# The last group of a factorization-machine kernel: rows of the result added into PSUM banks, the last block copied by ScalarE, four stores in place of three

## The chip, the cores and the metric

One Trainium2 chip, one of its cores. The metric is the time of one execution on the device in microseconds (us); lower is better. Before the change the median of 3 runs is 777.99 us (777.85 to 778.26).

## The reference, cut to what matters

```python
B, N, H, L = (2048, 512, 1024, 8)          # x is r_x, (2048, 512), float32
s = jnp.einsum('bn,hln->bhl', x, beta)
ssq = jnp.einsum('bn,hln->bhl', x * x, beta * beta)
fm = 0.5 * jnp.sum(s * s - ssq, axis=-1)
linear_out = x @ W.T + b
return fm + linear_out
```

The output has 2048 rows and 1024 columns, float32.

## The kernel before, in words

The work is ten passes, each a product of x (or x squared) with a matrix of 512 rows and 1024 columns: one pass for W, eight for beta (a chunk of 128 values of h with their eight l each), and a last one, pass 9 (`Q_PASS`), for x squared times the sums of beta squared over l, scaled by -0.5. A pass takes the 2048 rows in eight pairs of 128-row blocks (`PAIRS`). One pair in one pass is a *group* `g`; there are 80 groups, and the last pass holds groups 72 (`FIRST_Q`) to 79 (`GROUPS - 1`).

A group is one multiplication of 2 x 2 blocks by seven block products and not eight. The two row blocks and the two 512-column halves give four result blocks, called 11, 12, 21 and 22 (row block first). Each float32 operand is split into a high and a low part (`t_hi`, `t_lo`, `s_hi`, `s_lo`), and each product is three matmuls of the parts times two halves of the contraction (`KP`), so six matmuls (lines 442, 446 and 448) of 128 x 128 by 512 columns. A group has 42 of them.

The products of a group use four PSUM banks, one set for even and one for odd groups. TensorE makes, in this order, P5 in bank E, P7 in bank D, P1 in bank A, P6 in bank B, and then adds three more onto banks that are kept: P3 onto E, P4 onto D, P2 onto A (`start` is False there, so the matmul accumulates). The helper `whole(g, place, s_op, t_op, start)` issues one product. The waits of TensorE ahead of P3, P4 and P2 say that whoever needed P5, P7 and P1 alone has taken them. The semaphores `p5_made`, `p7_made` and so on tell that a product is finished. With R2 = P1 + P6 (`add_r2`, line 804, from ScalarE's copy `r1` of P1, line 606, and bank B) the blocks are:

- 11 = bank A at its end (P1 + P2)
- 12 = bank E at its end (P5 + P3) + R2
- 21 = bank D at its end (P7 + P4) + R2
- 22 = P5 + P7 + R2

In the last pass the other nine passes' result is already in a buffer `f` in SBUF (`f_at(i)`, i = g - 72; for the last two groups it lies in the tile `cs`), two rows of blocks by 1024 columns, and each group adds its four blocks onto `f` and stores `f` to `out`. For groups 73 to 78 VectorE does, in this order: P5 onto `f` 22 (line 904), P7 onto `f` 22 (line 908), R2 (line 804), block 11 of the group before (`add_o11`, line 838), bank E onto `f` 12 (line 924), bank D onto `f` 21 (line 928). GpSimd, which does not read PSUM, adds R2 onto `f` 12, 21 and 22 (lines 987, 988, 996). The additions of VectorE at 924 and 928 wait for GpSimd's at 987 and 988. In the last group, 79, VectorE does GpSimd's two itself (lines 919 and 920), GpSimd does only 22 (line 996), and block 11 (line 838) comes after everything else.

SyncE issues all transfers. `store_rows(g)` stores block 12 (256 KB, line 347), then the row 21 and 22 in one (512 KB, line 350), then block 11 (256 KB, line 352), each after the semaphore of its sum; at its end SyncE waits until all stores have landed. In the last group SyncE, ScalarE and GpSimd have nothing else to do but what is named here; ScalarE's last instruction is the copy of P1 into `r1`.

The order of work on each engine is written out by hand as the order of the instructions in its block; nothing plans it at run time.

Of the kernel before, what the change touches and what calls it, by code (L numbers as in the profile page):

```python
# [5 lines left out]
P = 128  # L6
B, N, H, L = 2048, 512, 1024, 8
COLS = 512
PAIRS = B // (2 * P)
# [25 lines left out]
GROUPS = PAIRS * (Q_PASS + 1)  # L35
# [24 lines left out]
def pair_of(g):  # L60
    return order_of(g // PAIRS)[g % PAIRS]
# [6 lines left out]
def count(g):  # L68

    return g - DIRECT + 1  # L70
# [45 lines left out]
def fm_layer(nc, x_p, beta_p, w_p, bias, out):  # L116
# [12 lines left out]
    with ExitStack() as ctx:  # L129
# [3 lines left out]
        def sem(name):  # L133
            return ctx.enter_context(nc.semaphore(name))
# [87 lines left out]
        f12_added = sem("f12_added")  # L222
        f21_added = sem("f21_added")
        o22_added = sem("o22_added")

        block = ctx.enter_context(nc.Block())

# [34 lines left out]
        def _(sp):  # L262
# [72 lines left out]
            def load_f(i):  # L335
                last = FIRST_Q - PAIRS + i
                sp.wait_ge(acc_stored[last % 2], 16 * ((last - FIRST_MAIN) // 2 + 1))
                if i >= 6:
                    sp.wait_ge(rows_summed, FIRST_Q - FIRST_MAIN - 1 + i % 2)
                sp.dma_start(f_at(i), acc_kept.rearrange("(t p) h -> p t h", p=P)[:, 2 * i:2 * i + 2, :]  # L340
                             ).then_inc(f_loaded[i], 16)

            def store_rows(g):
                i, rows = g - FIRST_Q, 2 * pair_of(g) * P
                f = f_at(i)
                sp.wait_ge(c12_added, count(g))
                sp.dma_start(out[rows:rows + P, COLS:], f[:, 0, COLS:]).then_inc(stored, 16)
                sp.wait_ge(c21_added, count(g))
                sp.wait_ge(o22_added, i + 1)
                sp.dma_start(out[rows + P:rows + 2 * P, :], f[:, 1, :]).then_inc(stored, 16)  # L350
                sp.wait_ge(o11_added, i + 1)
                sp.dma_start(out[rows:rows + P, 0:COLS], f[:, 0, 0:COLS]).then_inc(stored, 16)
# [60 lines left out]
            for g in range(FIRST_Q, GROUPS):  # L413
# [11 lines left out]
                    load_f(5 + i)  # L425
                if i:
                    store_rows(g - 1)
            store_rows(GROUPS - 1)
            sp.wait_ge(stored, 48 * PAIRS)

        @block.tensor
        def _(pe):
# [18 lines left out]
            def whole(g, place, s_op, t_op, start):  # L451

                n = g // PAIRS
                for k in range(KP):
                    ready = t_split_place(n, t_op, k) if g % PAIRS == 0 or g <= DIRECT else None
                    made = product(bank(g, place), slot_of(g), s_op, t_hi[:, n % 2, t_op, :, :],
                                   t_lo[:, n % 2, t_op, :, :], k, start and k == 0, k == KP - 1, ready)
                return made
# [46 lines left out]
            for g in range(DIRECT, GROUPS):  # L505
                n, i = g // PAIRS, g % PAIRS
                if g in PREPARED:
                    pe.wait_ge(s_lo_ready, s_split_place(g))
                elif i >= HALF:
                    pe.wait_ge(s_loaded[slot_of(g)], 32 * (n if slot_of(g) >= 2 else n - 1))  # L510
                wait_bank(g, BANK_E)
                whole(g, BANK_E, S1, T1, True).then_inc(p5_made, 1)
                wait_bank(g, BANK_D)
                whole(g, BANK_D, S3, T3, True).then_inc(p7_made, 1)
                wait_bank(g, BANK_A)
                whole(g, BANK_A, A11, B11, True).then_inc(p1_made, 1)
                wait_bank(g, BANK_B)
                whole(g, BANK_B, S2, T2, True).then_inc(p6_made, 1)
                if g <= FIRST_Q:
                    pe.wait_ge(r5_copied, count(g))  # L520
                else:
                    pe.wait_ge(p5_taken, g - FIRST_Q)
                whole(g, BANK_E, S4, B22, False).then_inc(p3_made, 1)
                if g <= FIRST_Q:
                    pe.wait_ge(r7_copied, count(g))
                else:
                    pe.wait_ge(p7_taken, g - FIRST_Q)
                whole(g, BANK_D, A22, T4, False).then_inc(p4_made, 1)
                pe.wait_ge(r1_copied, count(g))
                whole(g, BANK_A, A12, B21, False).then_inc(p2_made, 1)  # L530

        @block.scalar
        def _(act):
# [56 lines left out]
            def square_x(g):  # L590
                act.wait_ge(x_loaded[slot_of(g)], x_loads(g))
                nc.scalar.activation(x_at(g)[:, 0:4, :], x_at(g)[:, 0:4, :], ACT.Square).then_inc(x_squared, 1)
# [95 lines left out]
            for g in range(FIRST_Q, GROUPS):  # L688
                for other in groups_for(SUMMED_IN, g):
                    split_s(other)  # L690
                copy_r1(g)
                for other in groups_for(SQUARED_IN, g):
                    square_x(other)

        @block.vector
        def _(dve):
# [196 lines left out]

            for g in range(FIRST_Q, GROUPS):
                i = g - FIRST_Q
                f = f_at(i)
                for other in groups_for(SUMMED_IN, g):
# [14 lines left out]
                add_r2(g)  # L914
                if i:
                    add_o11(g - 1)
                if g == GROUPS - 1:
                    dve.wait_ge(r2_added, count(g))
                    nc.vector.tensor_tensor(f[:, 0, COLS:], f[:, 0, COLS:], r2[:, :], ALU.add).then_inc(f12_added, 1)  # L919
                    nc.vector.tensor_tensor(f[:, 1, 0:COLS], f[:, 1, 0:COLS], r2[:, :], ALU.add  # L920
                                            ).then_inc(f21_added, 1)
                dve.wait_ge(p3_made, count(g))
                dve.wait_ge(f12_added, i + 1)
                nc.vector.tensor_tensor(f[:, 0, COLS:], bank(g, BANK_E), f[:, 0, COLS:], ALU.add
# [2 lines left out]
                dve.wait_ge(f21_added, i + 1)  # L927
                nc.vector.tensor_tensor(f[:, 1, 0:COLS], bank(g, BANK_D), f[:, 1, 0:COLS], ALU.add  # L928
                                        ).then_inc(c21_added, 1)
            add_o11(GROUPS - 1)  # L930

        @block.gpsimd
        def _(pool):
# [90 lines left out]
```

## Time and profile before

| | us |
|---|---|
| median of 3 runs | 777.99 (777.85 to 778.26) |
| the profiled execution | 779.09 |
| its span, first to last instruction | 777.3 |
| TensorE busy | 771.2 (99%) |
| VectorE busy | 572.2 (74%) |
| ScalarE busy | 395.2 (51%) |
| GpSimd busy | 343.3 (44%) |

The profile is of one execution. Its span runs from the first to the last instruction; what the execution takes beyond it, 1.8 us, lies around the instructions. In the rows PE is TensorE's matmul, PEld its loading of weights (beside the matmuls), DVE is VectorE, ACT ScalarE, POOL GpSimd, SPq the queue on which SyncE issues transfers. L904 is line 904. Matmul durations overlap: one starts 0.22 to 0.23 us after the other, and each is shown as 0.39 long. The granted clock of TensorE is full over the whole span.

### The profile page before, as it was taken

The numbers are of one execution on the slowest core, as the hardware profiler recorded it, in microseconds if no ns is written. First come the engines' busy times: TensorE is split into PE (matmuls) and PEld (weight loads), VectorE is DVE, ScalarE is ACT, GpSimd is POOL, SyncE is SP. The second block draws the span as 40 slices with busy tenths as digits, with TensorE's granted clock in tenths as the row PEclk, the third lists the DMA queues.
The fourth block names the chain that finished last, engine by engine and source line by source line (L and its number), as shares of the span: only waits on it lengthen the run. The fifth ranks groups of instructions, "written<-read, shape, count | busy, mean of one in ns | idle before, by whom it ended". The sixth has DMA issues, their size and how long they took to land.

```text
span 777.3 us, 9620 instructions
## 1 busy us (share of the span) xinstructions
PE 771.2 (99%) x3382; PEld 633.5 (82%) x3382; DVE 572.2 (74%) x582; ACT 395.2 (51%) x502; POOL 343.3 (44%) x264
## 2 busy tenths in 40 slices
PE   9999999999999999999999999999999999999997
PEld 5888888888888888888888888888888888888886
DVE  6898389968765876587658765876587659777776
ACT  5574356645554555455545554555455545552331
POOL 0144274445434643454346434543554367335332
PEclk9999999999999999999999999999999999999999
DMA  8697854185614660466046604651564155629823
GB/s 341 227 371 323 299 186 146 57 304 203 224 40 150 216 217 28 148 217 217 27 149 222 218 28 157 224 202 35 183 220 180 41 198 207 217 78 398 322 109 149
DMA packets 64017, 145.34 MB, mean 187 GB/s; under 512 B 4833, under 2 KB 41697, under 8 KB 61665
## 3 DMA queue, kind: packets, MB, share of 16 engines
q1 hardware_dynamic: 63968, 144.72, 52.1%
q8 instruction: 27, 0.44, 0.2%
q14 instruction: 22, 0.17, 0.1%
HBM read 102.76 MB, written 41.94 MB: 186 GB/s over the span
## 4 chain that ended last, share of the span: by engine, by line
PE 97%; DMA 1%; DVE 1%; issue 0%; SPq 0%; ACT 0%; DVEq 0%
PE bank L442 32%; PE bank L446 32%; PE bank L448 32%; DMA s_lo_in<-x_p 1%; DVE cs L919 0%; DVE s_lo L793 0%; PE bank L474 0%; ACT s_hi L588 0%; SPq L277 0%; DVE cs L838 0%; DVE cs L928 0%; DVEq L129 0%; PE bank L470 0%; PE bank L467 0%; SPq L265 0%
## 5 line engine op out<-in xcount | busy, mean ns | idle before, releaser
L446 PE MATMUL bank<-t_lo,s_hi 128*128 128x512 f32 x1116 | 434.3, 389 | 0.0
L442 PE MATMUL bank<-t_hi,s_hi 128*128 128x512 f32 x1108 | 431.6, 390 | 0.0
L448 PE MATMUL bank<-t_hi,s_lo 128*128 128x512 f32 x1108 | 431.1, 389 | 0.0
L446 PEld LDWEIGHTS bank<-t_lo,s_hi 128*128 128x128 f32 x1116 | 209.5, 188 | 43.3
L442 PEld LDWEIGHTS bank<-t_hi,s_hi 128*128 128x128 f32 x1108 | 208.0, 188 | 44.4 <-DVE t_hi_in L904 0.6
L448 PEld LDWEIGHTS bank<-t_hi,s_lo 128*128 128x128 f32 x1108 | 208.0, 188 | 43.3
L825 DVE TENSOR_REDUCE sums<-cs 128x256 f32<-128x2048 f32 x64 | 146.3, 2286 | 120.3 <-issue 86.0
L963 POOL TENSOR_TENSOR r<-r 128x512 f32<-128x512 f32 x70 | 94.9, 1356 | 262.1 <-ACT r L618 262.1
L967 POOL TENSOR_TENSOR cs<-r 128x512 f32<-128x512 f32 x70 | 93.9, 1341 | 117.7 <-issue 115.7
L626 ACT ACTIVATE cs<-bank 128x512 f32<-128x512 f32 x64 | 38.3, 598 | 203.5 <-PE bank L448 203.5
L701 DVE TENSOR_TENSOR t_lo<-t_lo_in,t_hi 128x1024 fp32r<-128x1024 f32 x63 | 107.9, 1717 | 0.0
L634 ACT ACTIVATE cs<-cs 128x1536 f32<-128x1536 f32 x64 | 95.5, 1492 | 0.0
L936 POOL TENSOR_TENSOR t_lo_in<-t_lo_in 128x1024 f32<-128x1024 f32 x32 | 79.0, 2469 | 0.1
L816 DVE TENSOR_TENSOR cs<-bank,r 128x512 f32<-128x512 f32 x70 | 48.3, 690 | 33.4 <-PE bank L448 33.2
L535 ACT CAST t_hi<-t_lo_in 128x1024 fp32r<-128x1024 f32 x63 | 65.7, 1047 | 3.7 <-DVE t_lo_in L717 2.9
L612 ACT COPY r<-bank 128x512 f32<-128x512 f32 x71 | 41.7, 587 | 49.5 <-PE bank L448 48.8
L804 DVE TENSOR_TENSOR r<-bank,r 128x512 f32<-128x512 f32 x78 | 53.4, 684 | 10.9 <-PE bank L448 10.7
L585 ACT CAST s_hi<-s_lo_in 128x1792 fp32r<-128x1792 f32 x16 | 27.2, 1698 | 67.3 <-DVE s_lo_in L783 67.3
L606 ACT COPY r<-bank 128x512 f32<-128x512 f32 x78 | 45.9, 588 | 28.0 <-PE bank L448 28.0
L810 DVE TENSOR_TENSOR cs<-bank,r 128x512 f32<-128x512 f32 x70 | 48.4, 691 | 8.1 <-PE bank L448 2.5
L974 POOL TENSOR_TENSOR acc<-acc,bias_all 128x256 f32<-128x256 f32 x64 | 49.0, 765 | 5.2 <-DMA acc<-acc_kept 5.2
L618 ACT COPY r<-bank 128x512 f32<-128x512 f32 x71 | 41.0, 577 | 3.5 <-PE bank L448 3.4
(66 smaller groups left out, 317.4 us busy)
## 6 DMA issues: line engine op xcount, KB each, us to landing
s_hi<-s_hi_kept SPq DMA_DIRECT2D x30, 896.0 KB, 5.0
s_lo<-s_lo_kept SPq DMA_DIRECT2D x30, 896.0 KB, 7.0
t_lo_in<-beta_p SPq DMA_DIRECT2D x16, 1024.0 KB, 7.2
s_lo_in<-x_p SPq DMA_DIRECT2D x17, 512.0 KB, 6.2
acc_kept<-cs SPq DMA_DIRECT2D x16, 512.0 KB, 4.8
acc<-acc_kept SPq DMA_DIRECT2D x64, 128.0 KB, 5.4
acc_kept<-acc SPq DMA_DIRECT2D x64, 128.0 KB, 1.8
s_hi_kept<-s_hi SPq DMA_DIRECT2D x8, 896.0 KB, 6.0
```

The source lines that it names most:

```text
L442: nc.tensor.matmul(to, s_hi[:, slot, s_op, cols], hi[:, k, :], start=start, stop=False, skip_group_check=True)
L446: nc.tensor.matmul(to, s_hi[:, slot, s_op, cols], lo[:, k, :], start=False, stop=False, skip_group_check=True)
L448: return nc.tensor.matmul(to, s_lo[:, slot, s_op, cols], hi[:, k, :], start=False, stop=stop, skip_group_check=True)
L535: nc.scalar.copy(t_hi[:, n % 2, op, ks, :], t_at(n, op)[:, ks, :]).then_inc(t_hi_ready, 1)
L634: nc.scalar.activation(squares_at(g)[:, COLS:], squares_at(g)[:, COLS:], ACT.Square).then_inc(squared, 1)
L701: nc.vector.tensor_tensor(t_lo[:, n % 2, op, ks, :], t_at(n, op)[:, ks, :], as_f32(t_hi[:, n % 2, op, ks, :]), ALU.subtract).then_inc(t_lo ...
L804: nc.vector.tensor_tensor(r2[:, :], bank(g, BANK_B), r1[:, :], ALU.add).then_inc(r2_added, 1)
L825: nc.vector.tensor_reduce(sums[:, :, :].rearrange("p r h -> p (r h)"), squares_at(g).rearrange("p (h l) -> p h l", l=L), AX_X, ALU.add).th ...
L936: nc.gpsimd.tensor_tensor(t_at(n, op), t_at(n, left), t_at(n, right), ALU.subtract).then_inc(t_summed, 1)
L963: nc.gpsimd.tensor_tensor(r5[:, :], r5[:, :], r7[:, :], ALU.add).then_inc(r57_added, 1)
L967: nc.gpsimd.tensor_tensor(cs[:, g % 2, 1, 1, :], r5[:, :], r2[:, :], ALU.add).then_inc(c22_added, 1)
L974: nc.gpsimd.tensor_tensor(acc[:, g % 2, :, :], acc[:, g % 2, :, :], part, ALU.add).then_inc(acc_biased, 1)
```

## The change

Only the last group, 79, changes. VectorE's loop over the last pass ends one group earlier, and the last group is written out:

- block 11 of group 78 is added first;
- P5 is added onto `f` 22 as before, and then `f` 12 is added into bank E (`raise_bank`), where P5 still stands; TensorE waits for that ahead of P3 (`e_raised`);
- P7 is added onto `f` 22 as before, and `f` 21 is added into bank D, ahead of P4 (`d_raised`);
- after R2 (which waits until `r1` has been copied) `f` 11 is added into bank A, ahead of P2 (`a_raised`);
- when P3 is done, `f` 12 is bank E + R2; when P4 is done, `f` 21 is bank D + R2. Lines 919 and 920 fall away;
- when P2 is done, bank A is block 11 of the output, and ScalarE copies it to `f` 11 (`o11_copied`).

SyncE stores the last group in four stores of 256 KB each, in the order 22, 12, 21, 11, with `store_last_rows`. GpSimd's code is as it was.

```diff
@@ -222,6 +222,10 @@
         f12_added = sem("f12_added")
         f21_added = sem("f21_added")
         o22_added = sem("o22_added")
+        e_raised = sem("e_raised")
+        d_raised = sem("d_raised")
+        a_raised = sem("a_raised")
+        o11_copied = sem("o11_copied")
 
         block = ctx.enter_context(nc.Block())
 
@@ -339,6 +343,19 @@
                     sp.wait_ge(rows_summed, FIRST_Q - FIRST_MAIN - 1 + i % 2)
                 sp.dma_start(f_at(i), acc_kept.rearrange("(t p) h -> p t h", p=P)[:, 2 * i:2 * i + 2, :]
                              ).then_inc(f_loaded[i], 16)
+
+            def store_last_rows():
+
+                i, rows = PAIRS - 1, 2 * pair_of(GROUPS - 1) * P
+                f = f_at(i)
+                sp.wait_ge(o22_added, i + 1)
+                sp.dma_start(out[rows + P:rows + 2 * P, COLS:], f[:, 1, COLS:]).then_inc(stored, 16)
+                sp.wait_ge(c12_added, count(GROUPS - 1))
+                sp.dma_start(out[rows:rows + P, COLS:], f[:, 0, COLS:]).then_inc(stored, 16)
+                sp.wait_ge(c21_added, count(GROUPS - 1))
+                sp.dma_start(out[rows + P:rows + 2 * P, 0:COLS], f[:, 1, 0:COLS]).then_inc(stored, 16)
+                sp.wait_ge(o11_copied, 1)
+                sp.dma_start(out[rows:rows + P, 0:COLS], f[:, 0, 0:COLS]).then_inc(stored, 16)
 
             def store_rows(g):
                 i, rows = g - FIRST_Q, 2 * pair_of(g) * P
@@ -425,8 +442,8 @@
                     load_f(5 + i)
                 if i:
                     store_rows(g - 1)
-            store_rows(GROUPS - 1)
-            sp.wait_ge(stored, 48 * PAIRS)
+            store_last_rows()
+            sp.wait_ge(stored, 48 * PAIRS + 16)
 
         @block.tensor
         def _(pe):
@@ -520,13 +537,19 @@
                     pe.wait_ge(r5_copied, count(g))
                 else:
                     pe.wait_ge(p5_taken, g - FIRST_Q)
+                if g == GROUPS - 1:
+                    pe.wait_ge(e_raised, 1)
                 whole(g, BANK_E, S4, B22, False).then_inc(p3_made, 1)
                 if g <= FIRST_Q:
                     pe.wait_ge(r7_copied, count(g))
                 else:
                     pe.wait_ge(p7_taken, g - FIRST_Q)
+                if g == GROUPS - 1:
+                    pe.wait_ge(d_raised, 1)
                 whole(g, BANK_D, A22, T4, False).then_inc(p4_made, 1)
                 pe.wait_ge(r1_copied, count(g))
+                if g == GROUPS - 1:
+                    pe.wait_ge(a_raised, 1)
                 whole(g, BANK_A, A12, B21, False).then_inc(p2_made, 1)
 
         @block.scalar
@@ -691,6 +714,8 @@
                 copy_r1(g)
                 for other in groups_for(SQUARED_IN, g):
                     square_x(other)
+            act.wait_ge(p2_made, count(GROUPS - 1))
+            nc.scalar.copy(f_at(PAIRS - 1)[:, 0, 0:COLS], bank(GROUPS - 1, BANK_A)).then_inc(o11_copied, 1)
 
         @block.vector
         def _(dve):
@@ -893,7 +918,7 @@
 
 
 
-            for g in range(FIRST_Q, GROUPS):
+            for g in range(FIRST_Q, GROUPS - 1):
                 i = g - FIRST_Q
                 f = f_at(i)
                 for other in groups_for(SUMMED_IN, g):
@@ -914,11 +939,6 @@
                 add_r2(g)
                 if i:
                     add_o11(g - 1)
-                if g == GROUPS - 1:
-                    dve.wait_ge(r2_added, count(g))
-                    nc.vector.tensor_tensor(f[:, 0, COLS:], f[:, 0, COLS:], r2[:, :], ALU.add).then_inc(f12_added, 1)
-                    nc.vector.tensor_tensor(f[:, 1, 0:COLS], f[:, 1, 0:COLS], r2[:, :], ALU.add
-                                            ).then_inc(f21_added, 1)
                 dve.wait_ge(p3_made, count(g))
                 dve.wait_ge(f12_added, i + 1)
                 nc.vector.tensor_tensor(f[:, 0, COLS:], bank(g, BANK_E), f[:, 0, COLS:], ALU.add
@@ -927,7 +947,32 @@
                 dve.wait_ge(f21_added, i + 1)
                 nc.vector.tensor_tensor(f[:, 1, 0:COLS], bank(g, BANK_D), f[:, 1, 0:COLS], ALU.add
                                         ).then_inc(c21_added, 1)
-            add_o11(GROUPS - 1)
+
+
+            g, i = GROUPS - 1, PAIRS - 1
+            f = f_at(i)
+
+            def raise_bank(place, row, columns, raised):
+                nc.vector.tensor_tensor(bank(g, place), bank(g, place), f[:, row, columns], ALU.add
+                                        ).then_inc(raised, 1)
+
+            left, right = slice(0, COLS), slice(COLS, 2 * COLS)
+            add_o11(g - 1)
+            dve.wait_ge(f_loaded[i], 16)
+            dve.wait_ge(p5_made, count(g))
+            nc.vector.tensor_tensor(f[:, 1, right], bank(g, BANK_E), f[:, 1, right], ALU.add).then_inc(p5_taken, 1)
+            raise_bank(BANK_E, 0, right, e_raised)
+            dve.wait_ge(p7_made, count(g))
+            dve.wait_ge(p5_taken, i)
+            nc.vector.tensor_tensor(f[:, 1, right], bank(g, BANK_D), f[:, 1, right], ALU.add).then_inc(p7_taken, 1)
+            raise_bank(BANK_D, 1, left, d_raised)
+            add_r2(g)
+            raise_bank(BANK_A, 0, left, a_raised)
+            dve.wait_ge(p3_made, count(g))
+            dve.wait_ge(r2_added, count(g))
+            nc.vector.tensor_tensor(f[:, 0, right], bank(g, BANK_E), r2[:, :], ALU.add).then_inc(c12_added, 1)
+            dve.wait_ge(p4_made, count(g))
+            nc.vector.tensor_tensor(f[:, 1, left], bank(g, BANK_D), r2[:, :], ALU.add).then_inc(c21_added, 1)
 
         @block.gpsimd
         def _(pool):
```

## Rows read from the trace of the kernel before

**Rows 1.** Page of the profile: busy time of TensorE, chain that ended last

```profile
PE 771.2 (99%) x3382; PEld 633.5 (82%) x3382; DVE 572.2 (74%) x582; ACT 395.2 (51%) x502; POOL 343.3 (44%) x264
...
PE 97%; DMA 1%; DVE 1%; issue 0%; SPq 0%; ACT 0%; DVEq 0%
```

**Rows 2.** Timeline, TensorE: start us, us, engine, line, operation

```profile
763.16 0.39 PE L448 MATMUL bank<-t_hi,s_lo 128*128 128x512 f32 x1
763.38 0.39 PE L442 MATMUL bank<-t_hi,s_hi 128*128 128x512 f32 x1
...
768.82 0.39 PE L442 MATMUL bank<-t_hi,s_hi 128*128 128x512 f32 x1
...
770.18 0.39 PE L442 MATMUL bank<-t_hi,s_hi 128*128 128x512 f32 x1
...
771.54 0.39 PE L442 MATMUL bank<-t_hi,s_hi 128*128 128x512 f32 x1
...
772.68 0.39 PE L448 MATMUL bank<-t_hi,s_lo 128*128 128x512 f32 x1
```

**Rows 3.** Timeline, VectorE, groups 78 and 79

```profile
765.65 0.69 DVE L928 TENSOR_TENSOR cs<-bank,cs 128x512 f32<-128x512 f32 x1 [0.56 <-POOL cs L988]
766.25 0.68 DVE L904 TENSOR_TENSOR cs<-bank,cs 128x512 f32<-128x512 f32 x1
...
769.02 0.69 DVE L804 TENSOR_TENSOR r<-bank,r 128x512 f32<-128x512 f32 x1 [1.29 <-PE bank L448]
769.63 0.68 DVE L838 TENSOR_TENSOR cs<-bank,cs 128x512 f32<-128x512 f32 x1
770.23 1.45 DVE L919 TENSOR_TENSOR cs<-cs,r 128x512 f32<-128x512 f32 x1
771.61 0.68 DVE L920 TENSOR_TENSOR cs<-cs,r 128x512 f32<-128x512 f32 x1
...
773.41 0.67 DVE L838 TENSOR_TENSOR cs<-bank,cs 128x512 f32<-128x512 f32 x1
```

**Rows 4.** Timeline, GpSimd and ScalarE, groups 78 and 79

```profile
765.50 1.30 POOL L996 TENSOR_TENSOR cs<-cs,r 128x512 f32<-128x512 f32 x1
769.85 1.28 POOL L996 TENSOR_TENSOR cs<-cs,r 128x512 f32<-128x512 f32 x1 [3.05 <-DVE r L804]
...
767.66 0.59 ACT L606 COPY r<-bank 128x512 f32<-128x512 f32 x1 [6.98 <-PE bank L448]
```

**Rows 5.** Timeline, DMA issues of SyncE (SPq)

```profile
765.12 0.33 SPq L347 DMA_DIRECT2D out<-cs  x1
766.87 0.33 SPq L350 DMA_DIRECT2D out<-cs  x1
770.34 0.33 SPq L352 DMA_DIRECT2D out<-cs  x1
772.91 0.33 SPq L347 DMA_DIRECT2D out<-cs  x1
773.51 0.33 SPq L350 DMA_DIRECT2D out<-cs  x1
774.11 0.33 SPq L352 DMA_DIRECT2D out<-cs  x1
```

**Rows 6.** DMA by window (765:766, 770.2:772, 774:777): KB each, us to landing

```profile
q8 instruction: 1, 0.02, 5.5%
...
out<-cs SPq DMA_DIRECT2D x1, 256.0 KB, 2.6
...
out<-cs SPq DMA_DIRECT2D x1, 256.0 KB, 2.0
...
out<-cs SPq DMA_DIRECT2D x1, 256.0 KB, 2.8
```

**Rows 7.** Busy time by window; last two columns: DMA share, GB/s

```profile
773.50:774.00 0.50, 0.00 (x0) 0.00 (x0) 0.50 (x1) 0.00 (x0) 0.00 (x0) 1.00 0.53 201
776.00:776.50 0.50, 0.00 (x0) 0.00 (x0) 0.00 (x0) 0.00 (x0) 0.00 (x0) 1.00 0.83 320
```

## The prediction

> **What bounds the kernel now.** I read the page first. TensorE is busy 771.2 us of 777.3 and holds 97% of the chain that ended last [rows 1]; its clock is full, so nothing but TensorE's own stream and what stands after its last matmul can move the time. The change touches only the last group (group 79 of 80), so the next view is the order of events of the last 15 us, engine by engine.
>
> TensorE runs one product (six matmuls) in 1.36 us: P3 of the last group starts at 768.82, P4 at 770.18, P2 at 771.54, and the last matmul starts at 772.68 and ends at 773.07 [rows 2]. The span ends at 777.3, so 4.2 us stand behind the matmuls. They are:
> - VectorE is late by half an operation. It issues one add of 512 columns every 0.60 us (770.23 is the exception), and its last one, O11, starts at 773.41 though TensorE was done at 773.07; it ends at 774.08 [rows 3].
> - SyncE issues the last store at 774.11, 0.03 after that [rows 5].
> - That store, 256 KB, is down 2.8 us after its issue, at 776.91 [rows 6], and 0.4 later the span ends. The 2.8 is not the store's own: the three stores of the last group are issued at 772.91, 773.51 and 774.11 [rows 5] and hold 1 MB. The DMA engines start between 773.5 and 774.0 and are still moving 320 GB/s from 776.0 to 776.5 [rows 7]. The same form of store, issued alone at 770.34, is down in 2.0 us [rows 5, 6].
>
> So the end is a queue: three stores within 1.2 us, then 1 MB of data in a row, then a landing.
>
> **The change, part by part.** First the removed work: the adds at L919 (1.45 us) and L920 (0.68), and O11 of the last group on VectorE (0.67) [rows 3]. In their place come three adds that write PSUM, `raise_bank` on E, D and A, and a copy on ScalarE. VectorE still has nine operations in the group, in another order.
>
> VectorE's new order, from 766.25, when the C21 add of group 78 (765.65) lets it go [rows 3]. Steps are 0.60 between independent adds:
> - O11 of group 78 at 766.25; its bank was finished before group 79's first matmul at 763.38 [rows 2], so it does not wait.
> - P5 into the 22 rows at 766.85, raise E at 767.45, done at 768.13.
> - P7 into the 22 rows at 768.05 (it waits for its own P5 add, over by 767.53), raise D at 768.65, done at 769.33.
> - `add_r2` at 769.25 to 769.93. It could start at 769.02 now (P6's end) [rows 3], so it is 0.23 late.
> - raise A at 769.85, done at 770.53.
> - C12 needs P3's end: P4 starts at 770.18, its predecessor's last matmul 0.22 before that and 0.39 long, so 770.35. C12 runs from 770.45 to 771.13.
> - C21 needs P4's end, 771.71: it runs from 771.74 to 772.42.
>
> TensorE's three new waits ask for E before 768.82, D before 770.18 and A before 771.54 [rows 2]. The margins are 0.69, 0.85 and 1.01 us, so they cost nothing. Nothing else is queued behind them but the matmuls themselves. The instruction of a wait costs nothing either: P5 of group 79 has two waits ahead of it as well and starts 0.22 after the matmul before, the usual step [rows 2]. If the margin were gone, each microsecond of delay would be a microsecond of time.
>
> The price of an add that writes a bank is in no row. From below it is bounded by the read of a bank on the other engine, 0.59 (L606) [rows 4]; from above by the slowest 512-column add here, 1.45 (L919, both inputs in SBUF beside GpSimd's add from 769.85) [rows 3, 4]. I take 0.68, the add at L904, which reads exactly these operands and which took 0.68 beside GpSimd too (766.25, GpSimd from 765.50 to 766.80). At 0.59 nothing changes, since the chain has slack; the end at 1.45 is the rival below.
>
> GpSimd's add of R2 into the 22 rows follows `add_r2`: 769.85 is 0.14 after 769.71 now, so it becomes 770.07 to 771.36 (1.28 to 1.30 long) [rows 3, 4]. It is 0.22 later than before, hidden, since its store is now the first of four.
>
> SyncE: the four stores. The 22 block follows GpSimd by 0.07 (766.80 to 766.87) [rows 4, 5]: 771.43. The 12 block right behind, about 771.8 (an issue takes 0.33). The 21 block at 772.42 + 0.03 = 772.45. The 11 block is what matters: ScalarE sees P1's end within 0.03 (P1's last matmul, 1.36 + 0.22 before 768.82, ends at 767.63; the copy starts at 767.66) and copies in 0.59 [rows 2, 4]. ScalarE has nothing else there. So 773.07 + 0.03 + 0.59 = 773.69, and the store is issued at 773.72, against 774.11: **0.39 us** less.
>
> The queue: 201 GB/s over the half microsecond from 773.5 are 0.10 MB, and 320 over that from 776.0 are 0.16 MB [rows 7]. If both are stretches at one full rate of r, the 1.05 MB fit between 774.0 - 0.10/r and 776.0 + 0.16/r: r is 0.79 MB in 2 us, 395 GB/s. So data start at 773.75, 0.84 us after the issue at 772.91, and 256 KB take 0.66 us. In the new order the first pair's 512 KB move from 772.27 to 773.6, the 21 block to 774.26, and the last store's data start at 774.56: the engines are free 0.3 us before. So it lands like the store issued alone, in 2.0 instead of 2.8 us: **0.76 us** less (2.04 against 2.8). The 2.8 holds a wait on other stores that no longer exists.
>
> The sum: 0.39 + 0.76 = **1.15 us**. Landing at 775.76, end of span 0.39 later at 776.15, against 777.3. The profiled execution took 779.09, 1.8 us outside its span; it would take 777.94. The median of the runs shown is 777.99, 1.10 lower than the profiled one, and goes to **776.8**.
>
> What the store takes is bounded too: 2.0 (the lone one) and 2.8 (in the queue), with 2.6 for the one at 765.12 that came upon other traffic [rows 5, 6]. With 2.6 the gain is 0.59, with 2.8 it is 0.39.
>
> The Trainium skill ("DMA: Bandwidth & Descriptors", section on the anatomy of one DMA) gives, for transfers on GpSimd's path, about 2.0 us fixed and the bytes at 436 GB/s. By that an estimate for 256 KB is 2.6 us, and the sum would come to 777.4. The row at 770.34 went below it.
>
> **The rivals.**
> 1. *The last store lands as late as one with company.* The stores ahead of it on the same 16 engines, or an instruction fetch, keep it at 2.6 to 2.8. For: the store of 765.12 took 2.6, and in its window the instruction queue moved one packet of 0.02 MB [rows 5, 6]; a fetch can fall on the last store too. Against: 770.34 at 2.0, and the free 0.3 us. It gives 777.99 - 0.39 to 0.59, so 777.4 to 777.6. The fit of the Trainium skill above is the same case by another road.
> 2. *Slower: the bank writes are slow and hold TensorE at P2.* Place: the wait for raise A ahead of P2. At 1.45 per raise (a step of 1.37) raise E is done at 768.9, raise D starts at 769.42, `add_r2` at 770.79, raise A at 771.39 and is done at 772.84. P2 starts there instead of at 771.54, 1.30 us late. Against the 1.15 gained that is +0.15: 778.1. It decides from a step of about 1.3 us; below 0.94 nothing of it shows. For slower by more than 0.2% (1.6 us) each raise would have to step by 1.8. For: no row shows a write to PSUM by VectorE. Against: every add with one input in a bank took 0.67 to 0.69 [rows 3], with GpSimd at work or not.
> 3. *More than counted.* The end of the span is also the end of all engines' blocks; VectorE is done at 772.4 instead of 774.08 and its part of the ending may shrink, or the store lands in under 2.0. That gives 776.2 to 776.5, and only its far end passes 0.2%. For: 0.4 us between landing and end of span is explained by no row. Against: SyncE is the one that waits for the landing.
> 4. *The adds into the banks don't stay* (the matmul that follows overwrites them). Then the output is another, but every instruction runs as counted, so the time is the forecast's.
>
> **How the numbers follow.** About 0.2% (1.6 us) is what a measurement of this kernel can tell from no change. Forecast with rival 4: 0.70, all of it within 0.2% (1.15 us is 0.15%) except where the two medians stray by 0.4 us, which their spread (777.85 to 778.26) makes a matter of 0.06. Rival 1: 0.14. Rival 3: 0.09, two thirds beyond 0.2%. Rival 2: 0.07, of which 0.04 beyond 0.2%. So faster 0.06 + 0.06 = 0.12, slower 0.04, same 0.84. The range takes the forecast with the runs' spread (0.4 us) below it, which holds the nearer part of rival 3, and rival 1 whole with half that spread above: 776.3 to 777.8.
>
> **What would show it.** Right: the last matmul still ends 4.2 - 1.15 = 3.1 us before the span's end; raises of 0.67 to 0.69; no idle time of TensorE ahead of P3, P4 or P2; ScalarE's copy 0.03 after the last matmul, the last store 0.6 after that, landing 2.0 later; DMA idle for a moment ahead of the last 256 KB. Wrong: a gap ahead of P2 that names VectorE's raise (rival 2), or a last store of 2.6 or more (rival 1), or an end of span less than 0.3 us behind the landing (rival 3). A change anywhere before 763 us would say that the program's layout matters, which nothing here accounts for.

## The result, and the profile after

Over 12 runs of each, the changed kernel takes 777.15 us (776.45 to 778.16) and the kernel before 778.5 us (777.85 to 779.81). The ratio is 0.9983, with a 95% interval of 0.9975 to 0.999, so 1.35 us less, between 0.8 and 1.9. The forecast was 776.8 in 776.3 to 777.8 and "within 0.2%" as the likeliest verdict; the ratio is 0.17% below 1.

The profiled execution took 776.45 us with a span of 774.7, which is 2.6 us less than the 777.3 of before. That is more than twice what was forecast, and it has two parts that have to be told apart. The first is the tail, from the end of the last matmul to the end of the span. I take the end of a 512-column matmul as its start + 0.39 throughout (+ 0.28 for one of 256 columns). The views print a span to 0.1 us, which is too coarse to tell tails apart, so the tails below are taken from the trace's own times, to 0.01 us (a difference from the printed spans can be 0.05 off).

Page of the changed kernel: busy time and the chain that ended last. They answer to [rows 1]; line numbers are 17 and more higher than before.

```profile
PE 770.4 (99%) x3382; PEld 634.4 (82%) x3382; DVE 570.5 (74%) x582; ACT 395.9 (51%) x503; POOL 343.4 (44%) x264
...
PE 99%; ACT 0%; DVE 0%; issue 0%
```

Timeline of the changed kernel, TensorE, as [rows 2]: the starts of P3, P4, P2 and of the last matmul.

```profile
767.36 0.39 PE L459 MATMUL bank<-t_hi,s_hi 128*128 128x512 f32 x1
...
768.72 0.39 PE L459 MATMUL bank<-t_hi,s_hi 128*128 128x512 f32 x1
...
770.08 0.39 PE L459 MATMUL bank<-t_hi,s_hi 128*128 128x512 f32 x1
...
771.21 0.39 PE L465 MATMUL bank<-t_hi,s_lo 128*128 128x512 f32 x1
```

Timeline of the changed kernel, VectorE, as [rows 3]. L863 is block 11 of group 78, L963 and L967 the P5 and P7 adds, L956 the three raises, L829 R2, L973 and L975 blocks 12 and 21.

```profile
764.83 0.68 DVE L863 TENSOR_TENSOR cs<-bank,cs 128x512 f32<-128x512 f32 x1
765.43 0.68 DVE L963 TENSOR_TENSOR cs<-bank,cs 128x512 f32<-128x512 f32 x1
766.03 0.69 DVE L956 TENSOR_TENSOR bank<-bank,cs 128x512 f32<-128x512 f32 x1
766.63 0.68 DVE L967 TENSOR_TENSOR cs<-bank,cs 128x512 f32<-128x512 f32 x1
767.23 0.69 DVE L956 TENSOR_TENSOR bank<-bank,cs 128x512 f32<-128x512 f32 x1
767.82 0.68 DVE L829 TENSOR_TENSOR r<-bank,r 128x512 f32<-128x512 f32 x1
768.42 0.69 DVE L956 TENSOR_TENSOR bank<-bank,cs 128x512 f32<-128x512 f32 x1
769.02 0.68 DVE L973 TENSOR_TENSOR cs<-bank,r 128x512 f32<-128x512 f32 x1
770.28 0.69 DVE L975 TENSOR_TENSOR cs<-bank,r 128x512 f32<-128x512 f32 x1 [0.58 <-PE bank L465]
```

Timeline of the changed kernel, ScalarE and then SyncE's issues, as [rows 4, 5].

```profile
771.64 0.59 ACT L718 COPY cs<-bank 128x512 f32<-128x512 f32 x1 [4.85 <-PE bank L465]
```

```profile
769.96 0.33 SPq L352 DMA_DIRECT2D out<-cs  x1
770.33 0.43 SPq L354 DMA_DIRECT2D out<-cs  x1
771.00 0.33 SPq L356 DMA_DIRECT2D out<-cs  x1
772.25 0.33 SPq L358 DMA_DIRECT2D out<-cs  x1
```

DMA of the changed kernel in the window 772.2:772.5 (KB, us to landing), as [rows 6], and busy time by window, as [rows 7].

```profile
out<-cs SPq DMA_DIRECT2D x1, 256.0 KB, 2.0
```

```profile
772.40:772.80 0.40, 0.00 (x0) 0.00 (x0) 0.00 (x0) 0.00 (x0) 0.00 (x0) 1.00 1.01 384
772.80:773.00 0.20, 0.00 (x0) 0.00 (x0) 0.00 (x0) 0.00 (x0) 0.00 (x0) 1.00 0.33 113
773.00:773.40 0.40, 0.00 (x0) 0.00 (x0) 0.00 (x0) 0.00 (x0) 0.00 (x0) 1.00 0.78 297
```

The last matmul ends at 771.21 + 0.39 = 771.60. ScalarE's copy starts 0.04 later and takes 0.59, the last store is issued 0.65 after the matmul, and it is down in 2.0 us. From 772.8 to 773.0 the DMA engines are mostly idle (113 GB/s), so the last 256 KB found them free. The span ends 3.07 us after the last matmul, against 4.24 before: **1.17 us**, the forecast's 1.15. The chain that ended last no longer holds VectorE's late adds; it is TensorE and then ScalarE's copy.

The second part is 1.47 us ahead of all that: the last matmul itself ends at 771.60 and not at 773.07. TensorE is busy without a break from 20 us to the last group in both traces, so most of the difference should be there from the start. The rows that show it are ScalarE's cast of the second half of the first pair's x, and its first copy of a result, in three profiles.

Timeline, ScalarE, first 15 us, of the kernel before:

```profile
7.50 0.62 ACT L588 CAST s_hi<-s_lo_in 128x512 fp32r<-128x512 f32 x1 [1.14 <-DMA s_lo_in<-x_p]
...
14.75 0.59 ACT L600 COPY cs<-bank 128x512 f32<-128x512 f32 x1 [0.86 <-PE bank L448]
```

The same of the changed kernel:

```profile
6.03 0.62 ACT L611 CAST s_hi<-s_lo_in 128x512 fp32r<-128x512 f32 x1
...
13.60 0.59 ACT L623 COPY cs<-bank 128x512 f32<-128x512 f32 x1 [1.22 <-PE bank L465]
```

And of the changed kernel once more (`after_again`, below):

```profile
7.80 0.62 ACT L611 CAST s_hi<-s_lo_in 128x512 fp32r<-128x512 f32 x1 [1.77 <-DMA s_lo_in<-x_p]
...
15.01 0.59 ACT L623 COPY cs<-bank 128x512 f32<-128x512 f32 x1 [1.02 <-PE bank L465]
```

The same program has its first copy at 13.60 in one profile and at 15.01 in another, where a load of x came later (the wait of 1.77 us ahead of the cast); its last matmul ends at 771.60 and 773.17, 758.0 and 758.2 us behind that copy (before: 773.07 - 14.75 = 758.3). So 1.15 of the 1.47 us stand at the first copy already. The other 0.3 lie behind it and are not the change's either: `before_again`, the kernel before once more, has its first copy at 14.14 and its last matmul 758.0 behind it.

A late load is not the only thing that moves the first copy. In `two_adds_ahead` the cast starts at 6.73, earlier than before's 7.50, and yet the first copy is at 15.44: its matmuls follow each other at 0.43 us instead of 0.23 up to 10.2 us (the granted clock is shown as full there, and no row says why). In `raises_three_stores` the cast starts at 7.80, as in `after_again`, but the first copy is at 16.83. TensorE stood 1.9 us there ahead of its matmul at 7.52, waiting for ScalarE, and from 9.4 to 12.7 its granted clock is at the lower of its two levels, 1.2 GHz, with ten matmuls at 0.43 us. Busy time by window of it (the 0.50 is the granted clock):

```profile
9.40:12.70 3.30, 3.30 (x10) 2.53 (x9) 2.81 (x3) 2.60 (x4) 0.00 (x0) 0.50 1.03 421
```

None of this touches the last group, but all of it is in the times.

### The profile page after: what moved, and what is told of

The parts are those of the page before. It is cut to its first block, busy times and chain, and to the rows that moved or that the text cites. A ratio compares the mean times of both kernels' runs of the same rounds, so it can differ in the third digit from the quotient of the medians.

```text
span 774.7 us, 9622 instructions
## 1 busy us (share of the span) xinstructions
PE 770.4 (99%) x3382; PEld 634.4 (82%) x3382; DVE 570.5 (74%) x582; ACT 395.9 (51%) x503; POOL 343.4 (44%) x264
## 4 chain that ended last, share of the span: by engine, by line
PE 99%; ACT 0%; DVE 0%; issue 0%
PE bank L459 33%; PE bank L463 33%; PE bank L465 33%; PE bank L452 1%; PE bank L484 0%; PE bank L487 0%; PE bank L491 0%; ACT cs L718 0%; DVE r L722 0%
## 5 line engine op out<-in xcount | busy, mean ns | idle before, releaser
L829 DVE TENSOR_TENSOR r<-bank,r 128x512 f32<-128x512 f32 x78 | 53.4, 684 | 10.0 <-PE bank L465 9.8
```

The lines of the kernel that those rows point to most:

```text
L829: nc.vector.tensor_tensor(r2[:, :], bank(g, BANK_B), r1[:, :], ALU.add).then_inc(r2_added, 1)
```

## The experiments

Beside the ratio of times, each kernel is put in two numbers that the first 15 us touch less: the tail of its profile, and the shortest span among its runs beside the shortest among the runs of the kernel before that were taken together with them.

| kernel | last matmul ends | tail | shortest span, before's | ratio of times (95%) |
|---|---|---|---|---|
| before | 773.07 | 4.24 | | |
| before_again | 772.14 | 4.25 | | |
| changed kernel | 771.60 | 3.07 | 774.5 | 0.9983 (0.9975 to 0.999) |
| after_again | 773.17 | 3.08 | 774.6, 775.8 | 0.9978 (0.997 to 0.9987) |
| after_third | 771.69 | 3.07 | 774.8, 775.6 | 0.9985 (0.9973 to 0.9997) |
| four_stores_only | 773.15 | 3.63 | 775.3, 775.8 | 0.9994 (0.9986 to 1.0003) |
| raises_three_stores | 774.87 | 3.18 | 774.8, 775.8 | 0.9993 (0.9983 to 1.0002) |
| two_adds_ahead | 774.23 | 3.24 | 775.5, 775.8 | 0.9993 (0.9982 to 1.0004) |
| vector_adds_11 | 772.18 | 3.19 | 774.8, 775.7 | 0.9996 (0.9986 to 1.0005) |
| two_copies_two_stores | 771.60 | 3.20 | 774.8, 775.7 | 0.9988 (0.9979 to 0.9998) |
| p2_in_halves | 772.07 | 3.00 | 774.3, 775.7 | 0.999 (0.9982 to 0.9999) |
| p4_last_in_halves | 772.35 | 2.90 | 775.2, 775.6 | 0.9988 (0.9977 to 1.0) |

Every interval of the last column holds what the tail says, less what TensorE lost in the variants that hold it up, but five of the seven variants' intervals also reach 1: the ratios don't tell the variants apart, and the verdicts below rest on the tails. Those are one profile each; only the kernel before (4.24, 4.25) and the changed kernel (3.07, 3.08, 3.07) were profiled more than once, and they repeat within 0.01 us.

**The same kernels again.** `after_again` and `after_third` are the changed kernel, `before_again` the one before; no edit.

> The changed kernel once more. The tail, from the end of the last matmul (its start + 0.39) to the end of the span, was 4.24 us before and 3.11 in the one profile of the changed kernel; the place of the last matmul itself was 1.47 us earlier too (771.60 against 773.07). Theory 1: the change is worth its tail, 1.13 us, and the other 1.4 us are when the first loads arrive, which varies from run to run whatever the kernel. Then the tail is 3.1 again, and the last matmul may end anywhere from 771.5 to 773.2. Theory 2: the new program is also earlier ahead of the last group; then the last matmul ends near 771.6 again, and the time is 2.4 us below before.

> The kernel before once more, one look. The profiles so far place the end of the last matmul at 773.07 (before), 771.60 and 773.17 (the same changed kernel twice), 773.15 and 774.87. Theory 1 (that place varies with the arrival of the first loads, the tail is fixed by the program): tail 4.2 again, and a last matmul anywhere from 771.5 to 775. Rival (before is always about 773.1): 773.1 and 4.2.

> The changed kernel a third time, beside the run above on the same chip: tail 3.0 to 3.1, a last matmul anywhere between 771.5 and 775, the shortest span of its runs 1.1 to 1.2 us below the shortest span of before's runs, which is the tail's gain freed from the arrival of the first loads.

Theory 1 held in each: tails of 3.08 and 3.07 against 4.24 and 4.25, and last matmuls ending anywhere between 771.6 and 773.2, for the kernel before too (772.14 and 773.07). What it says of the first loads is half of the matter, as the rows of the first 15 us above show. The shortest spans differ by 1.2 us beside `after_again` and by 0.8 beside `after_third`, which is the expected 1.1 to 1.2 in the first only. So the change is worth its tail.

**The two halves of the change apart.** `four_stores_only` is the kernel before with the new function for the stores (22, 12, 21, 11), whose last wait is on `o11_added`:

```diff
@@ block.sync, kernel before @@
-            store_rows(GROUPS - 1)
-            sp.wait_ge(stored, 48 * PAIRS)
+            store_last_rows()
+            sp.wait_ge(stored, 48 * PAIRS + 16)
```

> The kernel before with its last group stored by four stores (22, 12, 21, 11) and VectorE's work as it was. Theory 1 (a queue of stores is what the last landing waits for, and VectorE's lateness makes the queue): the 22 block leaves at about 771.3 on before's clock, 12, 21 and 11 still at 772.9, 773.5 and 774.1, so 0.75 MB instead of 1 MB stand in the queue. Its data run from 773.75 to 775.7, the last landing comes 0.6 to 0.7 us earlier than before and the tail is 3.6. Rival (only the late issue of the last store counts, its 2.8 us are its own): tail 4.24 as before.

Timeline of `four_stores_only`, SyncE, and DMA of the window 774.15:774.3:

```profile
771.24 0.33 SPq L348 DMA_DIRECT2D out<-cs  x1
772.99 0.33 SPq L350 DMA_DIRECT2D out<-cs  x1
773.59 0.33 SPq L352 DMA_DIRECT2D out<-cs  x1
774.19 0.33 SPq L354 DMA_DIRECT2D out<-cs  x1
```

```profile
out<-cs SPq DMA_DIRECT2D x1, 256.0 KB, 2.2
```

The last store leaves 1.04 us after the last matmul (773.15), as before, but is down in 2.2 us and not 2.8: the 22 block was out of the way. Tail 3.63, as expected; the queue was real, and 0.6 us of it goes without touching VectorE.

`raises_three_stores` is the other half, the changed kernel with the three stores of before:

```diff
@@ store_last_rows, changed kernel @@
-                sp.wait_ge(o22_added, i + 1)
-                sp.dma_start(out[rows + P:rows + 2 * P, COLS:], f[:, 1, COLS:]).then_inc(stored, 16)
                 sp.wait_ge(c12_added, count(GROUPS - 1))
...
                 sp.wait_ge(c21_added, count(GROUPS - 1))
-                sp.dma_start(out[rows + P:rows + 2 * P, 0:COLS], f[:, 1, 0:COLS]).then_inc(stored, 16)
+                sp.wait_ge(o22_added, i + 1)
+                sp.dma_start(out[rows + P:rows + 2 * P, :], f[:, 1, :]).then_inc(stored, 16)
```

> The changed kernel with the three stores of before (12; the row of 21 and 22; 11). Theory 1: with the raises the row leaves at 0.65 us after P4's end, 1.28 us ahead of the last store, and its 512 KB (1.3 us of data) are through just as the last store's data start; the tail is that of the changed kernel, 3.1 to 3.2, so the fourth store is worth nothing once the raises are there. Rival (the fourth store is what frees the queue): tail 3.5 to 3.8.

Timeline of `raises_three_stores`, SyncE:

```profile
772.96 0.33 SPq L352 DMA_DIRECT2D out<-cs  x1
774.26 0.39 SPq L355 DMA_DIRECT2D out<-cs  x1
775.52 0.33 SPq L357 DMA_DIRECT2D out<-cs  x1
```

DMA of the windows 774.2:774.4 and 775.5:775.7:

```profile
out<-cs SPq DMA_DIRECT2D x1, 512.0 KB, 2.7
...
out<-cs SPq DMA_DIRECT2D x1, 256.0 KB, 2.1
```

The row of 512 KB leaves 1.26 us ahead of the last store and takes 1.3 us of data, so the last store is down in 2.1 us. Tail 3.18, against 3.07 with four. The last matmul ends late, at 774.87, in part for the lower clock between 9.4 and 12.7 us (above), which the tail doesn't see, and its shortest span is 1.0 us under before's. Two of its twelve runs took 968.83 us (mean granted clock 0.753) and 2783.47 us; they are not in the ratio, and why the second took so long is open. So the two halves don't add: with VectorE's sums on time, the fourth store is worth 0.1 us.

One more number of this profile bears on the forecast's rival 1. The store of block 12 leaves at 772.96 with no other store near it, and is down in 2.9 us; the instruction queue moved one packet in the window 773:774. So it was with the store of 765.12 in the kernel before (2.6 us, [rows 6]). Issued alone and without such a packet beside it, a store of 256 KB was down in 2.0 us there (770.34). That the packet is the cause is not shown, only that they stand together.

**Which engine finishes block 11.** `vector_adds_11`:

```diff
@@ changed kernel @@
-                if g == GROUPS - 1:
-                    pe.wait_ge(a_raised, 1)
...
-            act.wait_ge(p2_made, count(GROUPS - 1))
-            nc.scalar.copy(f_at(PAIRS - 1)[:, 0, 0:COLS], bank(GROUPS - 1, BANK_A)).then_inc(o11_copied, 1)
...
-            raise_bank(BANK_A, 0, left, a_raised)
...
+            add_o11(g)
```

> The changed kernel without the raise of bank A and without ScalarE's copy: VectorE adds block 11 as in the kernel before, now with nothing ahead of it. Theory 1 (what was gained in front of the last store is VectorE's lateness of 0.34 us, the other engine gives only the shorter operation): the add starts 0.04 after the last matmul as ScalarE's copy did, takes 0.67 to 0.69 and not 0.59, the last store leaves at +0.74 instead of +0.65, tail 3.15 to 3.2. Rival (the copy of a bank by ScalarE is what counts, the first add on VectorE after TensorE's last matmul being late for another reason): add at +0.3, tail 3.4.

Timeline of `vector_adds_11`, VectorE:

```profile
772.22 0.69 DVE L859 TENSOR_TENSOR cs<-bank,cs 128x512 f32<-128x512 f32 x1 [0.67 <-PE bank L465]
```

VectorE's add starts 0.04 after the last matmul and takes 0.69: the last store leaves at +0.76 and the tail is 3.19. Raising bank A and giving the last block to ScalarE is worth 0.1 us; the other 1.05 is VectorE having nothing left to do when P2 ends, which the raises of E and D bring, with the 0.1 of the fourth store in it.

**The margin of the new waits.** `two_adds_ahead`:

```diff
@@ last group on VectorE, changed kernel @@
+            dve.wait_ge(f22_added, 1)
+            nc.vector.tensor_tensor(r5[:, :], bank(g, BANK_E), f[:, 1, left], ALU.add)
+            nc.vector.tensor_tensor(r7[:, :], bank(g, BANK_E), f[:, 1, left], ALU.add)
             raise_bank(BANK_E, 0, right, e_raised)
```

> The changed kernel with two adds of 512 columns (bank and SBUF into a spare tile) on VectorE ahead of raise E, 1.2 us in all; nothing is left out of the result. It tests the margin of TensorE's new waits. By the profile of the changed kernel raise E is done 0.64 us before P3 starts (766.72 against 767.36), so with 1.2 us more TensorE must stand 0.55 to 0.6 us ahead of P3, and once only: D and A then keep margins of 0.2 to 0.4. Theory 1: one gap of 0.55 us ahead of P3, tail 3.1, time 0.55 above the changed kernel. Rival (the waits have more room than the rows say, or TensorE makes up for a gap): no difference.

Timeline of `two_adds_ahead`, the raise of E and the first matmul of P3:

```profile
769.06 0.69 DVE L956 TENSOR_TENSOR bank<-bank,cs 128x512 f32<-128x512 f32 x1
```

```profile
769.90 0.47 PE L459 MATMUL bank<-t_hi,s_hi 128*128 128x512 f32 x1 [0.53 <-DVE bank L956]
```

One gap, ahead of P3 and put down to the raise, 0.69 us (0.92 from one start to the next instead of 0.23) and none ahead of P4 and P2. It is 0.1 longer than expected, because TensorE started 0.15 after the raise's end (769.75) and I had counted nothing for that. Behind the gap the second matmul follows after 0.31 us and not 0.23, so TensorE loses 0.78 in all (from P3's first to the last matmul it takes 3.94 us, against 3.85 in the changed kernel). A second effect was not expected: the tail grew to 3.24. R2 and GpSimd's 22 block came late too, so the stores of 22, 12 and 21 left at -1.24, -0.87 and -0.39 and the last one took 2.2 us. The slack of the changed kernel's end is thus some 0.5 us at P3, and less than that in the queue of stores.

**Can the tail be shorter still?** Three versions cut the last block in two. `two_copies_two_stores` does it behind the matmul:

```diff
@@ ScalarE, changed kernel; the store of block 11 is cut in two the same way @@
-            nc.scalar.copy(f_at(PAIRS - 1)[:, 0, 0:COLS], bank(GROUPS - 1, BANK_A)).then_inc(o11_copied, 1)
+            for half in range(2):
+                cols = slice(256 * half, 256 * half + 256)
+                nc.scalar.copy(f_at(PAIRS - 1)[:, 0, cols], bank(GROUPS - 1, BANK_A)[:, cols]).then_inc(o11_copied, 1)
```

> The changed kernel with ScalarE's copy of block 11 cut into two of 256 columns and its store into two of 128 KB. The issue to landing of 256 KB is 2.0 us, of which 0.66 are data at 395 GB/s. Theory 1: copies at +0.04 and about +0.32 (ScalarE's copies of half the columns take some 0.37), stores at about +0.45 and +0.82 (an issue right behind another one takes 0.38 here), the second with 128 KB and thus 0.33 us less of data: down at +2.5, tail 2.9 to 3.0. Rival (a landing costs the same whatever its size, and the extra copy and issue come on top): tail 3.2 to 3.3.

DMA of `two_copies_two_stores`, windows 772.0:772.2 and 772.42:772.7 (the two last stores), and its copies:

```profile
out<-cs SPq DMA_DIRECT2D x1, 128.0 KB, 1.9
...
out<-cs SPq DMA_DIRECT2D x1, 128.0 KB, 2.0
```

```profile
771.64 0.65 ACT L722 COPY cs<-bank 128x256 f32<-128x256 f32 x2 [4.85 <-PE bank L467]
```

The rival was right: 128 KB are down 1.9 to 2.0 us after their issue, as 256 KB are. The second store leaves later than the one store did (+0.81, not +0.65) and gains nothing back: tail 3.20.

`p2_in_halves` lets TensorE finish one half while the other leaves:

```diff
@@ last group, changed kernel @@
-                whole(g, BANK_A, A12, B21, False).then_inc(p2_made, 1)
+                for half, place in enumerate((BANK_A, BANK_B)):
+                    part = slice(256 * half, 256 * half + 256)
...
+                            made = nc.tensor.matmul(bank(g, place)[:, part], left_in[:, slot, A12, cols],
+                                                    right_in[:, k, part], start=False,
...
+                    made.then_inc(p2_made, 1)
...
-            raise_bank(BANK_A, 0, left, a_raised)
+            nc.vector.tensor_tensor(bank(g, BANK_A)[:, 0:256], bank(g, BANK_A)[:, 0:256], f[:, 0, 0:256], ALU.add
+                                    ).then_inc(a_raised, 1)
+            nc.vector.tensor_tensor(bank(g, BANK_B)[:, 256:512], bank(g, BANK_A)[:, 256:512], f[:, 0, 256:512],
+                                    ALU.add).then_inc(a_raised, 1)
```

> The changed kernel with P2 of the last group made in two halves of 256 columns, the left onto bank A and the right onto bank B (free since R2; its rows are raised there from bank A), each copied by ScalarE and stored by itself, so that half of block 11 leaves while TensorE still works on the other half. Behind the last matmul there are then a copy of 256 columns (some 0.37) and a store of 128 KB (2.0 - 0.33): tail about 2.55, 0.5 less. What P2 costs in halves is open: theory 1, the loading of weights (0.19 us a time in the rows, two thirds of it beside matmuls) stays hidden and 12 matmuls of half the columns take 1.4 to 1.5 instead of 1.36 us, so the kernel is 0.4 us faster than the changed one; rival, the weights set the pace at 0.19 us each, P2 takes 2.3 us and the kernel is 0.4 us slower than the changed one.

Timeline of `p2_in_halves`, TensorE: the first three and the last matmul of P2.

```profile
770.48 0.28 PE L565 MATMUL bank<-t_hi,s_hi 128*128 128x256 f32 x1
770.59 0.28 PE L565 MATMUL bank<-t_lo,s_hi 128*128 128x256 f32 x1
770.71 0.28 PE L565 MATMUL bank<-t_hi,s_lo 128*128 128x256 f32 x1
...
771.79 0.28 PE L565 MATMUL bank<-t_hi,s_lo 128*128 128x256 f32 x1
```

Busy time of it by window:

```profile
771.40:773.00 1.60, 0.67 (x6) 0.47 (x4) 0.00 (x0) 0.73 (x2) 0.00 (x0) 1.00 1.03 384
773.00:773.40 0.40, 0.00 (x0) 0.00 (x0) 0.00 (x0) 0.00 (x0) 0.00 (x0) 1.00 0.97 341
773.40:773.80 0.40, 0.00 (x0) 0.00 (x0) 0.00 (x0) 0.00 (x0) 0.00 (x0) 1.00 1.03 343
773.80:774.20 0.40, 0.00 (x0) 0.00 (x0) 0.00 (x0) 0.00 (x0) 0.00 (x0) 1.00 0.62 208
```

The weights stayed hidden: matmuls of 256 columns follow each other by 0.12 us, so P2 costs 0.07 us more. The copy took 0.37. But the second half store, issued at 772.50, is down only 2.2 us later, where 1.67 was expected (2.0 - 0.33). Two things are in that. Half the bytes gain nothing, as `two_copies_two_stores` showed (1.9 to 2.0 us). The other 0.2 to 0.3 is the queue again: the engines were busy without a break from the 22 block on (384, 341, 343 GB/s up to 773.8). The tail is 3.00, 0.07 less than the changed kernel's, and after the 0.07 of TensorE nothing is left.

`p4_last_in_halves` reorders the last group's products so that R2 and the 22 block come earlier, and halves P4 instead. GpSimd adds R2 onto `f` 22 first here, and VectorE adds P7 behind it:

```
last group on TensorE
-P5  P7  P1  P6  P3  P4  P2
+P5  P1  P6  P7  P3  P2  P4 (left half onto D, right half onto B)
```

> A version meant to beat both. In the run with P2 in halves the halves cost 0.07 us of TensorE and the copy behind the last matmul took 0.37, but the last 128 KB came 2.2 us after their issue, because the 1 MB of the last group had kept the DMA engines busy since the 22 block. Here the products of the last group come in the order P5, P1, P6, P7, P3, P2, P4, so R2 and with it the 22 block are ready one product earlier, and P4 is the one in halves (left onto D, right onto B). By the rows (products of 1.36, adds at steps of 0.60, GpSimd's add 1.3) the stores leave at about -2.6 (22), -2.0 (12), -0.8 (11), -0.3 (left of 21) and +0.5 (right of 21) from the last matmul's end, so the engines are free before the last one. Theory 1: the last 128 KB are down 1.75 us after their issue and the tail is 0.5 + 1.75 + 0.4 = 2.65, with no gap of TensorE ahead of P3, P2 or P4; together with the 0.07 the time is 0.4 us below the changed kernel's. Rival (a store's landing has a floor that its size does not lower): down in 2.0, tail 2.9, no gain beyond 0.1 to 0.2 us.

Timeline of `p4_last_in_halves`: VectorE's P7 add, the raises of D and B, and P4's first matmul.

```profile
769.04 0.69 DVE L1000 TENSOR_TENSOR cs<-bank,cs 128x512 f32<-128x512 f32 x1 [0.92 <-POOL cs L1081]
769.84 0.76 DVE L1005 TENSOR_TENSOR bank<-bank,cs 128x256 f32<-128x256 f32 x2
```

```profile
770.66 0.39 PE L545 MATMUL bank<-t_hi,s_hi 128*128 128x256 f32 x1 [0.21 <-DVE bank L1005]
```

It failed on the point that I had not worked out: VectorE waits for GpSimd's 22 add (until 769.04) and raises D and B in 0.76 us, done at 770.60, while P4 could have started at 770.29. TensorE starts it 0.06 after the raise, 0.37 late, and loses 0.10 more on the next matmul (0.22 from one start to the other, where 0.12 is usual). The last 128 KB are down 2.0 us after their issue, behind the three stores ahead of it, which is the rival's figure, but not with free engines. The tail is 2.90, 0.17 shorter; the gap and the halves cost TensorE some 0.5, so more is lost than gained, and its shortest span (775.2) is 0.4 above that of the changed kernel beside it (`after_third`, 774.8). Of the two, only `p2_in_halves` has a shorter shortest span than the changed kernel (774.3 against 774.5 to 774.8), which its ratio does not confirm. No version beats the changed kernel for sure.

## Why the prediction was right

- *The order of the new group.* Forecast, counted from the last matmul's end: stores at -1.64, -1.27, -0.62 and +0.65. Measured: -1.64, -1.27, -0.60 and +0.65. The steps of 0.60 and GpSimd's place behind R2 held.
- *The bank writes.* Taken as 0.68 between bounds of 0.59 and 1.45; measured 0.69 (L956), three times. TensorE has no gap ahead of P3, P4 or P2. Rival 2 is out. The forecast's margins of 0.69, 0.85 and 1.01 us came out as 0.64, 0.80 and 0.97, and what was left out of them is the handover to TensorE, 0.15 us in `two_adds_ahead` and 0.06 in `p4_last_in_halves`.
- *The 0.39 of the late VectorE.* Measured 1.04 - 0.65 = 0.39. `vector_adds_11` splits it: its store leaves at +0.76, so 0.28 is VectorE's lateness and 0.11 the shorter copy.
- *The 0.76 of the queue.* The last store was down in 2.0 instead of 2.8 us. The DMA engines were nearly idle from 772.8 to 773.0 (113 GB/s), some 0.2 us where 0.3 were forecast. The first half of rival 1, company on the engines, is out for this order of stores. That the queue was the cause and not a landing's own length is shown by `four_stores_only`, where the same late store took 2.2. Its second half, an instruction fetch that falls on the last store, was met in no profile and is therefore not refuted: a packet of that queue stood beside a store that took 2.9 us in `raises_three_stores`, only not beside the last one.
- *The sum.* 1.15 forecast, 1.17 in the tail (4.24 to 3.07; again 3.08 and 3.07), 1.35 (0.8 to 1.9) in the times. That the time itself came as near as 777.15 to 776.8 is in part luck: the median of the kernel before, from which the forecast subtracts, rose from 777.99 to 778.5 with more runs, and the difference in the times is 0.2 above the forecast's; the two errors go against each other.
- *Rival 3*, a shorter end behind the landing: the span ended 0.4 us after the last landing before and after. It is out.
- *Rival 4* was set at the forecast's own time, so no time here tells it from the forecast. The values do: the changed kernel's output is the reference's, which it could not be if P3, P4 and P2 had overwritten the rows added into the banks. It is out.

What was mis-sized is the spread. The prediction took 777.85 to 778.26 as the runs' spread and derived from it a chance of 0.06 that two medians stray by 0.4 us. Over 12 runs the kernel before goes from 777.85 to 779.81. This scatter is nearly twice the effect. Where the profiles show it, it stands in the first 15 us, in the arrival of the first loads and in how long TensorE goes at 0.43 us a matmul; how the runs without a profile divide between the two is open. The three ratios of the changed kernel (0.9978, 0.9983, 0.9985) lie on both sides of 0.2%. The chance for "faster by over 0.2%" should have been well above 0.12.

## What to carry to other kernels

Behind the last matmul count three things: how late each engine is with what it owes by then, the length of the last operation, and the bytes that earlier stores still have in the DMA queue when the last store's data could start. They hide each other: either half of this change alone gave 0.6 or 1.1 us, both together 1.2. Where the effect is a microsecond and the first 15 us scatter by two or three, measure the stretch that the change touches, from a mark ahead of it to the end, and use whole times only to confirm.

## What the runs showed of the hardware

- A VectorE add that reads a bank and an SBUF tile and writes the bank takes 0.69 us for 512 columns, the same as with an SBUF destination (0.68), also beside GpSimd (L956 at 768.42, GpSimd from 768.64).
- A store's time to land hardly follows its size when it is small: 2.0 us for 256 KB, 1.9 and 2.0 for 128 KB. The 128 KB stores have rows of 1 KB instead of 2 KB and moved at about 340 GB/s, where the stores of 256 KB moved at 384.
- Matmuls of 256 columns with a weight load each follow at 0.12 us, though a load is shown as 0.19 us long.
- An add of VectorE that TensorE waits for is followed by the matmul 0.15 us after its end (`two_adds_ahead`) or 0.06 (`p4_last_in_halves`), and the matmul after that comes 0.1 us later than the usual step.
- The first loads of the same program land at other times from run to run: its first copy of a result stood at 13.60 and at 15.01 us, and everything behind moved with it.
- The granted clock can be at its lower level early in a program: 9.4 to 12.7 us in `raises_three_stores`, ten matmuls at 0.43 us, first copy at 16.83 us.
